# Attention with a look-ahead term and an FFN on one core: all rows of the squared pairs' probabilities turned by VectorE's squares and DRAM

## Chip, cores and metric

One core of a Trainium2 chip. The metric is the device time of one launch in microseconds, the median of several runs; lower is better. The engines are TensorE (matmuls and transposes, into PSUM), VectorE, ScalarE and GpSimd (elementwise work; GpSimd does not touch PSUM here) and SyncE, whose queue issues the DMA transfers. In the profile they are PE (PEld for its weight loads), DVE, ACT, POOL and SP (SPq for its queue). Each runs its own program in order and waits on semaphores.

## The reference

A layer norm, then attention with a look-ahead term and a gated FFN side by side, both added to x. There are 8 batches of 512 tokens of 256 features, 8 heads of 64.

```python
xn = _layernorm(x)
qu, ku, vu, qc, kc, vc = split_heads(xn @ W_qkv.T)      # 6 x (8, 8, 512, 64)
term1 = where(causal_mask, 0, (qc * SCALE) @ vu.T)
lookahead = where(causal_mask, sigmoid((qu * SCALE) @ ku.T), 0)
Su = term1 @ lookahead.T
scores = where(causal_mask, neg, (qc * SCALE) @ kc.T - silu(Su))
out = softmax(scores) @ vc
x = x + merge_heads(out) @ W_out.T + ffn(xn)            # ffn: silu(x @ wg) * (x @ wu) @ wd, hidden 768
```

## The kernel before, in words

Numbers are split in two parts of fewer bits each, HIGH and LOW (ScalarE copies a value to the rounded type, VectorE subtracts the copy from the value), and a product of two split numbers is three matmuls.

The attention is a pipeline of 32 **steps**, one for each pair of heads of a batch: step g = 4b + q. The function `step` exists once for each engine and is an order of work written out by hand. In step g TensorE computes, for pair g, the look-ahead products L (`look_ahead`), term1 T (`term1`) and their product Su (`sum_up`); for pair g-1 the scores (`scores`); for pair g-2 the output (`attend`); and the projections of pair g+1. The causal triangle of a head is cut in three groups, `ROWS = [(4,), (3, 1), (2,)]`: the row block of four 128-column blocks, then those of three and of one, then that of two. Each of L, T, scores and Su goes by these groups, j = 0, 1, 2.

What happens to pair g-1 in step g, row group by row group: VectorE forms minus the scores from PSUM and the gate and takes their least (`minus_scores`, L1487), into the tile `prob`; ScalarE takes the exponential and its sum (`exp_of`, L1176); VectorE the inverse of the sum (`inverse`, L1499); GpSimd multiplies by it (`norm`, L668). `attend` then wants these probabilities with keys along the partitions, that is transposed, split in HIGH and LOW, in the tile `PT_s`. There are two ways to this:

- The last row block (four blocks of columns, both heads) of the pairs below `SQUARED` = 30 goes by **squares and DRAM**: VectorE transposes every 32 x 32 square in place (`row_in_squares`, L1527), SyncE spreads the squares to DRAM (`spread_last_row`, L545, eight DMAs of 64 KB in pieces of 128 B), waits for them, and gathers them back as transposed blocks (L552, four DMAs). In the next step ScalarE and VectorE split them (`high_last_row`, L1204; `low_last_row`, L1533).
- The other three row blocks of these pairs are transposed by TensorE, six 128 x 128 transposes for a head (`turn_head`, L867), between the sums: one head behind sum 0 and one behind sum 1. ScalarE (`high_head`, L1196, L1198) and VectorE (`low_head`, L1521) split them out of PSUM behind the gate and its product of the same sum.

The last two pairs are turned wholly by TensorE (`turn_probs`, L842).

**The tail of a step.** TensorE runs sum 0, a head's transposes, sum 1, the other head's, sum 2. For each sum ScalarE takes a tanh (`gate_of`, L1168) and VectorE a product with the sum (`silu_of`, L1471), which frees the sum's banks in PSUM. Ahead of this VectorE has the LOW parts of L (`low_L`, L1457), of the projections (`low_proj`, L1419) and of the values (`low_values`, L1424), and by q: at q = 0 the statistics of the next x, at q = 1 its scaling and its transpose by squares, at q = 2 the LOW part of xT, at q = 3 nothing of these (a plain step). The weights of the FFN are split in chunks in steps 4 to 25.

**The banks.** PSUM has 8 banks, and `TURNS` lists which banks each piece of work takes, in the order in which TensorE takes them. `take_bank` makes TensorE wait until what was in them before is emptied. Sum 0 has banks 6 and 7, which the next step's first T takes; sum 1 has 2 and 3, which the first L takes.

```python
TURNS = [("Sc", 0, (0, 1)), ("L", 0, (2, 3)), ("K0", 0, (0,)), ("T", 0, (6, 7)), ("L", 1, (4, 5)), ("T", 1, (2, 3)),
```

`attend` of a pair below `SQUARED` waits for the LOW parts of a head (L878) and of the last row (L879). SyncE's program in a step is, in order: the spread of x at q = 2, the store and the load of a weight chunk, the loads of q = 0, then at the end the last row's spread and gathers and the store of the output of pair g-2. The loads for the FFN stand in the last two steps; the last batch's xT is loaded in step 31 (L530).

After the steps comes the FFN of all batches with the output projection, on TensorE `gate_up`, `down` and `project_o`. The change touches no work of it but three banks and that load.

Of the kernel before, what the change touches and what calls it, by code (L numbers as in the profile page):

```python
# [103 lines left out]
class LayerNorm:  # L104
# [35 lines left out]
    def scale(self, dve, b):  # L140

        sh = self.sh
        for n in range(TT):
# [18 lines left out]
         ("Su", 0, (6, 7)), ("PH", 0, (0, 1)), ("PT", 0, (0, 1)), ("PT", 1, (4,)), ("Su", 1, (2, 3)),  # L162
         ("PH", 1, (6, 7)), ("PT", 2, (6, 7)), ("Su", 2, (4, 5))]
# [44 lines left out]
def layer(nc, x, W_qkv, w_gate, w_up, w_down, W_out, w_split, xT_copy, xT_raw, prob_raw, sh, heads_out, out):  # L208
# [4 lines left out]
    with ctx:  # L213
# [36 lines left out]
        flat_prob = prob[:, :, :].rearrange("p h c -> p (h c)")  # L250
        flat_T = T_s[:, :, :, :].rearrange("p h a c -> p (h a c)")
# [60 lines left out]
        last_row_in_squares = sem("last_row_in_squares")  # L312
        last_row_spread = sem("last_row_spread")
        last_row_loaded = sem("last_row_loaded")
        last_row_high = sem("last_row_high")
        last_row_low = sem("last_row_low")
# [48 lines left out]
        def gate_up_bank(b, m):  # L365

            if b > 0:
                return double[m % 2]
            return bank("GU", m) if m < 3 else double[(0, 0, 3)[m - 3]]
# [43 lines left out]
        def after(g, j):  # L413
            return g * 3 + j + 1

        def turned(g, n):
            return g * 2 + n + 1 if g < SQUARED else SQUARED * 2 + (g - SQUARED) * 3 + n + 1
# [34 lines left out]
        def run_steps(b, part, step, count=STEPS):  # L452


            for q in range(count):
                g = b * STEPS + q
                step(part, b, q, g, q >= 1 or part != FIRST, q >= 2 or part != FIRST, q < 3 or part != LAST)

        @block.sync
        def _(sp):  # L460
# [45 lines left out]
            def step(part, b, q, g, back1, back2, ahead):  # L506
# [19 lines left out]
                if part == LAST and q == 3:  # L526
                    sp.wait_ge(proj_filled, proj_count(LAST_G, KC))
# [11 lines left out]
            def spread_last_row(g, attended):  # L539

                sp.wait_ge(last_row_in_squares, g + 1)
                sp.sem_inc(ticks, 1)
                for h in range(2):
                    for i in range(4):
                        sp.dma_start(prob_raw[g][h].rearrange("q r t -> r q t")[:, :, i * 32:(i + 1) * 32],  # L545
                                     prob[i * 32:(i + 1) * 32, h, 0:SEQ].rearrange("r (q t) -> r q t", t=32)) \
                          .then_inc(last_row_spread, 16)
                sp.wait_ge(last_row_spread, (g + 1) * 8 * 16)
                if attended:
                    sp.wait_ge(o_filled, 2 * g)  # L550
                for K, at in enumerate((3, 6, 9, 7)):
                    sp.dma_start(PT_blocks[:, :, LOW, at, :],  # L552
                                 prob_raw[g][:, 4 * K:4 * K + 4, :, :].rearrange("h q r t -> (q r) h t")) \
                      .then_inc(last_row_loaded, 16)
# [81 lines left out]
        def _(pool):  # L636
# [25 lines left out]
            def norm(g, j):  # L662

                wait_before(pool, inv_done, after(g, j))
                for h in range(2):
                    for w in ROWS[j]:
                        v = prob[:, h, WIDE[w]:WIDE[w] + w * P]
# [60 lines left out]
        def _(pe):  # L728
# [109 lines left out]
            def turn_row(out, h, w):  # L838

                K = TT - w  # L840
                for I in range(K, TT):
                    last = pe.transpose(out[:, (I - K) * P:(I - K + 1) * P],  # L842
                                        prob[:, h, WIDE[I + 1] + K * P:WIDE[I + 1] + (K + 1) * P], ident[:, :])
# [17 lines left out]
            def turn_head(part, b, g, h):  # L861

                if h == 0:
                    pe.wait_ge(prob_ready, after(g - 1, 2))
                tile = take_bank(part, b, g, "PH", h)
                for i, (K, I) in enumerate([(0, 0), (0, 1), (0, 2), (1, 1), (1, 2), (2, 2)]):
# [949 lines left out]
```

## Time and profile before

| | us |
|---|---|
| three runs, median (lowest to highest) | 1081.72 (1080.22 to 1082.07) |
| the profiled execution, and its span | 1082.21, 1080.2 |
| busy in the span: TensorE, its weight loads | 1058.2, 947.6 |
| VectorE, ScalarE, GpSimd | 871.9, 755.8, 567.1 |
| packets of DMA, of these under 512 B | 246076, 161232 |

The span is from the first to the last instruction of the profiled execution. A matmul's record overlaps its neighbours', so that a row of TensorE is best read by the starts: the start of the next group less its own. An instruction of another engine can likewise start before the end recorded for the one ahead of it. The duration of a DMA issue is the time in the queue that issues it and not the time of the transfer. The granted TensorE clock was 0.996 of full speed.

### The profile page before, as it was taken

The numbers are of one execution on the slowest core, as the hardware profiler recorded it, in microseconds if no ns is written. First come the engines' busy times: TensorE is split into PE (matmuls) and PEld (weight loads), VectorE is DVE, ScalarE is ACT, GpSimd is POOL, SyncE is SP. The second block draws the span as 40 slices with busy tenths as digits, with TensorE's granted clock in tenths as the row PEclk, the third lists the DMA queues.
The fourth block names the chain that finished last, engine by engine and source line by source line (L and its number), as shares of the span: only waits on it lengthen the run. The fifth ranks groups of instructions, "written<-read, shape, count | busy, mean of one in ns | idle before, by whom it ended". The sixth has DMA issues, their size and how long they took to land.

```text
span 1080.2 us, 21562 instructions
## 1 busy us (share of the span) xinstructions
PE 1058.2 (98%) x7652; PEld 947.6 (88%) x7652; DVE 871.9 (81%) x1831; ACT 755.8 (70%) x1483; POOL 567.1 (52%) x630
## 2 busy tenths in 40 slices
PE   6999999999999999999999999999999899999998
PEld 5888888888888888888888889988889888899997
DVE  5788789888988898889888988888777768667766
ACT  6678777877787778777877787778777755443333
POOL 5355565556555655565556555656555545422230
PEclk9999999999999999999999999999999989999999
DMA  5032434343434343344334343433324546556631
GB/s 195 1 79 64 118 89 110 76 104 102 91 96 101 105 101 86 91 116 89 99 77 130 79 109 76 125 79 80 98 59 123 161 144 237 175 179 217 214 133 60
DMA packets 246076, 120.72 MB, mean 112 GB/s; under 512 B 161232, under 2 KB 227024, under 8 KB 243920
## 3 DMA queue, kind: packets, MB, share of 16 engines
q1 hardware_dynamic: 245968, 119.31, 40.5%
q8 instruction: 63, 1.03, 0.4%
q14 instruction: 45, 0.37, 0.1%
HBM read 64.75 MB, written 54.53 MB: 110 GB/s over the span
## 4 chain that ended last, share of the span: by engine, by line
PE 89%; DVE 3%; ACT 2%; issue 2%; POOL 1%; DMA 1%; SPq 1%; DVEq 0%; POOLq 0%; ACTq 0%
PE X L833 23%; PE X L748 20%; PE X L986 7%; PE X L885 7%; PE X L977 7%; PE X L817 6%; PE X L801 5%; PE X L787 5%; PE X L772 4%; PE X L867 4%; POOL prob L668 1%; DMA xT<-xT_copy 1%; DVE L_s L1457 1%; ACT prob L1176 1%; ACT T_s L1154 1%
## 5 line engine op out<-in xcount | busy, mean ns | idle before, releaser
L668 POOL TENSOR_SCALAR prob<-prob,inv 128x512 f32<-128x512 f32 (+3 forms) x256 | 301.4, 1194 | 16.3 <-DVE inv L1499 16.3
L833 PE MATMUL X<-L_s,T_s 128*128 128x128 f32 (+3 forms) x1920 | 281.7, 301 | 2.0 <-DVE L_s L1457 2.0
L833 PEld LDWEIGHTS X<-L_s,T_s 128*128 128x128 f32 x1920 | 267.5, 189 | 13.4 <-issue 2.8
L748 PE MATMUL X<-xT,W 128*128 128x512 f32 (+1 forms) x972 | 244.8, 399 | 0.0
L748 PEld LDWEIGHTS X<-xT,W 128*128 128x128 f32 x972 | 175.7, 191 | 40.8 <-issue 0.4
L1168 ACT ACTIVATE gate<-X 128x1024 f32<-128x1024 f32 (+1 forms) x96 | 84.9, 884 | 154.7 <-PE X L833 154.7
L642 POOL TENSOR_SCALAR_AFFINE_SELECT gate<-gate 128x256 f32<-128x256 f32 (+1 forms) x96 | 47.5, 495 | 205.2 <-DVE gate L1471 205.2
L1471 DVE SCALAR_TENSOR_TENSOR gate<-gate,X 128x1024 f32<-128x1024 f32 (+1 forms) x96 | 99.6, 1038 | 64.0 <-ACT gate L1168 64.0
L658 POOL TENSOR_SCALAR_AFFINE_SELECT T_s<-T_s 128x512 fp32r<-128x512 f32 x128 | 104.6, 829 | 85.4 <-DVE T_s L1464 85.4
L1176 ACT ACTIVATE prob<-prob,least 128x512 f32<-128x512 f32 (+3 forms) x256 | 141.8, 587 | 1.5 <-DVE least L1487 1.5
L1487 DVE CUSTOM_DVE_ANT_0 prob<-X,gate 128x512 f32<-128x512 f32 (+3 forms) x256 | 112.8, 487 | 25.8 <-PE X L817 24.2
L1464 DVE TENSOR_TENSOR T_s<-X,T_s 128x1024 fp32r<-128x1024 f32 (+1 forms) x96 | 100.1, 1043 | 28.9 <-ACT T_s L1154 28.9
L1457 DVE SCALAR_TENSOR_TENSOR L_s<-tanh_l,L_s 128x1024 fp32r<-128x1024 f32 (+1 forms) x96 | 104.0, 1083 | 0.5 <-ACT L_s L1160 0.5
L1146 ACT ACTIVATE tanh_l<-X 128x1024 f32<-128x1024 f32 (+1 forms) x96 | 85.5, 890 | 23.3 <-PE X L787 23.2
L885 PEld LDWEIGHTS X<-PT_s,v_s 128*128 128x128 f32 x512 | 80.8, 188 | 10.2 <-DVE PT_s L1512 1.5
L1154 ACT ACTIVATE T_s<-X 128x1024 fp32r<-128x1024 f32 (+1 forms) x96 | 85.8, 893 | 4.5 <-PE X L801 4.5
L885 PE MATMUL X<-PT_s,v_s 128*128 128x512 f32 (+3 forms) x512 | 85.2, 319 | 1.7 <-DVE PT_s L1512 1.1
L1160 ACT ACTIVATE L_s<-tanh_l 128x1024 fp32r<-128x1024 f32 (+1 forms) x96 | 85.6, 938 | 0.0
L817 PE MATMUL X<-kc_s,qc_s 64*128 64x512 f32 (+3 forms) x768 | 84.6, 337 | 0.0
L801 PE MATMUL X<-qc_s,vu_s 64*128 64x512 f32 (+3 forms) x768 | 81.8, 327 | 0.0
L650 POOL TENSOR_SCALAR_AFFINE_SELECT tanh_l<-tanh_l 128x256 f32<-128x256 f32 (+1 forms) x96 | 54.0, 563 | 51.1 <-ACT tanh_l L1146 51.1
L787 PE MATMUL X<-qu_s,ku_s 64*128 64x512 f32 (+3 forms) x768 | 79.5, 319 | 0.5 <-ACT tanh_l L1146 0.3
(108 smaller groups left out, 1888.2 us busy)
## 6 DMA issues: line engine op xcount, KB each, us to landing
heads_out<-o_s SPq DMA_DIRECT2D x62, 256.0 KB, 3.3
prob_raw<-prob SPq DMA_DIRECT2D x240, 64.0 KB, 1.9
PT_s<-prob_raw SPq DMA_DIRECT2D x120, 128.0 KB, 2.4
xT_copy<-xT SPq DMA_DIRECT2D x8, 1024.0 KB, 6.8
w_split<-w_parts SPq DMA_DIRECT2D x22, 256.0 KB, 2.5
W<-w_split SPq DMA_DIRECT2D x12, 384.0 KB, 6.9
xT<-xT_copy SPq DMA_DIRECT2D x4, 1024.0 KB, 6.3
tanh_l<-in_L_attn_x SPq DMA_DIRECT2D x8, 512.0 KB, 4.9
```

What stands on the lines that cost most here:

```text
L658: last = pool.affine_select(out=v, in_=v.bitcast(F32), compare_op=ALU.is_ge, fill=0.0, base=0, pattern=[[0, 2], [0, 2], [1, P]], channel_m ...
L668: last = pool.tensor_scalar(v, v, inv[:, h, w - 1:w], None, ALU.mult)
L748: last = pe.matmul(out[:, tokens], sh.W[:, a, k, cols], xT[:, c, k, tokens], start=(n == 0), stop=(n == 3 * KD - 1))
L787: last = pe.matmul(both[:, h, at:at + w * P], ku_s[rows, a, J * P:(J + 1) * P], qu_s[rows, c, 0:w * P], start=(n == 0), stop=(n == 2))
L801: last = pe.matmul(both[:, h, at:at + w * P], vu_s[rows, a, J * P:(J + 1) * P], qc_s[rows, q % 2, c, J * P:SEQ], start=(n == 0), stop=(n = ...
L817: last = pe.matmul(both[:, h, at:at + w * P], qc_s[rows, par, a, I * P:(I + 1) * P], kc_s[rows, par, c, 0:w * P], start=(n == 0), stop=(n ...
L833: last = pe.matmul(both[:, h, at:at + (J + 1) * P], T_s[:, h, a, to:to + P], L_s[:, h, c, WIDE[J + 1]:WIDE[J + 1] + (J + 1) * P], start=(J ...
L885: last = pe.matmul(both[:, h, K * P:SEQ], v_s[:, slot // 4, K, slot % 4, :, :], PT_s[:, h, c, at:at + (TT - K) * P], start=(K == 0 and c = ...
L1176: last = act.activation(v, v, ACT.Exp, bias=least[:, h, w - 1:w], scale=-1.0, accum_out=total[:, h, w - 1:w])
L1457: dve.scalar_tensor_tensor(L_s[:, :, LOW, c:c + n], tanh_l[:, :, c:c + n], 1.0, L_s[:, :, HIGH, c:c + n].bitcast(F32), ALU.add, ALU.subtra ...
L1464: dve.tensor_tensor(T_s[:, :, LOW, c:c + n], bank("T", j)[:, :, 0:n], T_s[:, :, HIGH, c:c + n].bitcast(F32), ALU.subtract).then_inc(T_low, 1)
L1487: last = dve.tensor_tensor_reduce(prob[:, h, WIDE[w]:WIDE[w] + w * P], both[:, h, at:at + w * P], gate[:, h, WIDE[w]:WIDE[w] + w * P], SU_ ...
```

## The change

For the pairs below `SQUARED` all four row blocks go by squares and DRAM. `turn_head`, `high_head` and `low_head` are gone, and with them TensorE's transposes and the banks `PH`. The tile `prob` is laid out so that both heads' parts of a row group lie side by side (`prob_row`, `prob_rows`): 1024 columns for row 3, 768 for row 2, and 768 for rows 1 and 0 together.

VectorE transposes the three groups in turn (`row_in_squares(g, I)` for I = 3, 2, 1), each behind its own norm, at three places in its order. SyncE spreads groups 3 and 2; **ScalarE** issues the spread of the third group (I = 1), between its first and its second gate. Each spread is four DMAs. SyncE gathers all of them, ten DMAs. ScalarE and VectorE split the whole of `PT_s` in two instructions each, 1280 columns for a head (`high_rows`, `low_rows`), where they split the last row before. Sum 0 now has banks 2 and 3, sum 1 has 6 and 7. VectorE's LOW parts of the projections QU and KU move behind those of L. The last batch's xT is loaded in step 30, and `double[1]` and `double[3]` change places in the first FFN stage.

```diff
-         ("Su", 0, (6, 7)), ("PH", 0, (0, 1)), ("PT", 0, (0, 1)), ("PT", 1, (4,)), ("Su", 1, (2, 3)),
-         ("PH", 1, (6, 7)), ("PT", 2, (6, 7)), ("Su", 2, (4, 5))]
+         ("Su", 0, (2, 3)), ("PT", 0, (0, 1)), ("PT", 1, (4,)), ("Su", 1, (6, 7)),
+          ("PT", 2, (2, 3)), ("Su", 2, (4, 5))]
...
+        def prob_row(h, w):
+            return flat_prob[:, 2 * WIDE[w] + h * w * P:2 * WIDE[w] + (h + 1) * w * P]
+
+        def prob_rows(I):
+            return flat_prob[:, 1792:2 * TRI] if I == 1 else flat_prob[:, 2 * WIDE[I + 1]:2 * (WIDE[I + 1] + (I + 1) * P)]
...
+        def spread_row(eng, g, I):
+
+            eng.wait_ge(row_in_squares_done[I], g + 1)
+            eng.sem_inc(ticks, 1)
+            to = prob_raw[I][g].rearrange("q r t -> r q t")
+            for i in range(4):
+                eng.dma_start(to[:, :, i * 32:(i + 1) * 32],
+                             prob_rows(I)[i * 32:(i + 1) * 32, :].rearrange("r (q t) -> r q t", t=32)) \
+                  .then_inc(row_spread[I], 16)
...
                 if part == LAST and q == 3:
+                    load_down_out()
+                if part == LAST and q == 2:
+                    load_gate_up()
                     sp.wait_ge(proj_filled, proj_count(LAST_G, KC))
                     sp.wait_ge(v_filled, LAST_G + 1)
                     sp.wait_ge(xT_stored, BATCH * 16)
                     load_xT(0)
-                    load_down_out()
-                if part == LAST and q == 2:
-                    load_gate_up()
                 if back1 and g - 1 < SQUARED:
-                    spread_last_row(g - 1, back2)
+                    for I in (3, 2):
+                        spread_row(sp, g - 1, I)
+                    if back2:
+                        sp.wait_ge(o_filled, 2 * g - 2)
+                    for I in (3, 2, 1):
+                        gather_row(g - 1, I)
                 if back2:
                     store_o(g - 2, q % 2)
...
+            def gather_row(g, I):
+
+                sp.wait_ge(row_spread[I], (g + 1) * 4 * 16)
+                for i in (I, 0) if I == 1 else (I,):
+                    for K in range(i + 1):
+                        sp.dma_start(PT_blocks[:, :, LOW, WIDE[TT - K] // P + i - K, :], raw_row(g, i)[:, 4 * K:4 * K + 4, :, :].rearrange("h q r t -> (q r) h t")) \
+                          .then_inc(row_loaded[I], 16)
...
                     if g - 2 < SQUARED:
-                        pe.wait_ge(PT_low, turned(g - 2, h))
-                        pe.wait_ge(last_row_low, 2 * (g - 2) + 2)
+                        pe.wait_ge(rows_low, 2 * (g - 2) + h + 1)
...
                 sum_up(part, b, g, 0)
-                if back1 and g - 1 < SQUARED:
-                    turn_head(part, b, g, 0)
-                elif back1:
+                if back1 and g - 1 >= SQUARED:
                     turn_probs(part, b, g, 0)
                     turn_probs(part, b, g, 1)
                 sum_up(part, b, g, 1)
-                if back1 and g - 1 < SQUARED:
-                    turn_head(part, b, g, 1)
-                elif back1:
+                if back1 and g - 1 >= SQUARED:
                     turn_probs(part, b, g, 2)
                 sum_up(part, b, g, 2)
...
+            def high_rows(g):
+
+                for I in (3, 2, 1):
+                    act.wait_ge(row_loaded[I], (g + 1) * (I + 1 if I > 1 else 3) * 16)
+                for h in range(2):
+                    act.activation(PT_s[:, h, HIGH, :], PT_plain[:, h, LOW, :], ACT.Copy).then_inc(rows_high, 1)
...
                 if back2 and g - 2 < SQUARED:
-                    high_last_row(g - 2)
+                    high_rows(g - 2)
...
                 gate_of(g, 0)
                 if back1 and g - 1 < SQUARED:
-                    high_head(g - 1, 0)
-                elif back1:
+                    spread_row(act, g - 1, 1)
+                if back1 and g - 1 >= SQUARED:
                     high_PT(g - 1, 0)
                     high_PT(g - 1, 1)
                 gate_of(g, 1)
...
+                if 0 <= g - 1 < SQUARED:
+                    for I in ((3,), (2, 1), (1,))[j]:
+                        wait_before(dve, row_spread[I], g * 4 * 16)
...
+            def row_in_squares(g, I):
+
+                dve.wait_ge(prob_ready, after(g, 3 - I))
+                dve.transpose(prob_rows(I), prob_rows(I)).then_inc(row_in_squares_done[I], 1)
+
+            def low_rows(g):
+
+                for h in range(2):
+                    dve.wait_ge(rows_high, 2 * g + h + 1)
+                    dve.tensor_tensor(PT_s[:, h, LOW, :], PT_plain[:, h, LOW, :], PT_plain[:, h, HIGH, :], ALU.subtract) \
+                       .then_inc(rows_low, 1)
...
                 if back1:
                     inverse(g - 1, 1)
-                if ahead:
-                    low_proj(g + 1, QU, par)
                 low_L(g, 1)
-                if ahead:
-                    low_proj(g + 1, KU, par)
...
                 if back1:
                     inverse(g - 1, 2)
+                if ahead:
+                    low_proj(g + 1, QU, par)
+                    low_proj(g + 1, KU, par)
                 if back1 and g - 1 < SQUARED:
-                    row_in_squares(g - 1)
+                    row_in_squares(g - 1, 3)
                 if ahead:
                     low_proj(g + 1, VU, par)
+                if back1 and g - 1 < SQUARED:
+                    row_in_squares(g - 1, 2)
...
+                if back1 and g - 1 < SQUARED:
+                    row_in_squares(g - 1, 1)
                 if 0 <= g - FIRST_CHUNK < INT_CHUNKS:
                     take_low_max(g - FIRST_CHUNK)
```

## Rows read from the trace of the kernel before

**Rows 1.** The page, engines: busy us (share of the span) xinstructions.

```profile
PE 1058.2 (98%) x7652; PEld 947.6 (88%) x7652; DVE 871.9 (81%) x1831; ACT 755.8 (70%) x1483; POOL 567.1 (52%) x630
```

**Rows 2.** The waits: who waited for whom, us in total, times, longest.

```profile
PE X L977 <- DMA xT<-xT_copy: 3.6, 1, 3.6
```

**Rows 3.** TensorE's timeline over one plain step: start us, us, what.

```profile
421.59 0.97 PE L817 MATMUL X<-kc_s,qc_s 64*128 64x512 f32 x6
...
439.06 3.95 PE L833 MATMUL X<-L_s,T_s 128*128 128x512 f32 x24
442.84 0.84 PE L867 MATMUL X<-ident,prob 128*128 128x128 f32 x6
443.44 3.30 PE L833 MATMUL X<-L_s,T_s 128*128 128x384 f32 x24
446.58 0.84 PE L867 MATMUL X<-ident,prob 128*128 128x128 f32 x6
...
448.67 0.96 PE L817 MATMUL X<-kc_s,qc_s 64*128 64x512 f32 x6
...
450.20 0.96 PE L801 MATMUL X<-qc_s,vu_s 64*128 64x512 f32 x6
```

**Rows 4.** Windows: length, busy us by engine (x), PEclk, DMA share, GB/s.

```profile
448.67:475.74 27.07, 27.07 (x203) 24.28 (x202) 23.70 (x58) 20.95 (x42) 16.75 (x19) 1.00 0.52 142
475.74:503.04 27.30, 27.23 (x204) 24.34 (x204) 24.72 (x54) 20.96 (x42) 15.76 (x18) 1.00 0.28 65
```

**Rows 5.** Groups by line and shape: busy us, mean ns | idle before.

```profile
L1457 DVE SCALAR_TENSOR_TENSOR L_s<-tanh_l,L_s 128x1024 fp32r<-128x1024 f32 x64 | 82.3, 1285 | 0.5 <-ACT L_s L1160 0.5
...
L1160 ACT ACTIVATE L_s<-tanh_l 128x1024 fp32r<-128x1024 f32 x64 | 65.0, 1085 | 0.0
...
L1527 DVE STREAM_TRANSPOSE prob<-prob 128x1024 f32<-128x1024 f32 x30 | 36.6, 1220 | 0.0
```

**Rows 6.** VectorE's timeline: last row's split, tails and gate products of three steps.

```profile
431.54 1.53 DVE L1533 TENSOR_TENSOR PT_s<-PT_s 128x768 fp32r<-128x768 f32 x2
...
438.06 0.68 DVE L1457 SCALAR_TENSOR_TENSOR L_s<-tanh_l,L_s 128x512 fp32r<-128x512 f32 x1
...
442.31 0.39 DVE L1439 TENSOR_REDUCE low_max<-w_parts 128x1 f32<-128x256 f32 x1
...
447.90 1.22 DVE L1471 SCALAR_TENSOR_TENSOR gate<-gate,X 128x1024 f32<-128x1024 f32 x1 [1.58 <-ACT gate L1168]
449.04 1.02 DVE L1521 TENSOR_TENSOR PT_s<-X,PT_s 128x512 fp32r<-128x512 f32 x2
...
471.73 1.21 DVE L1471 SCALAR_TENSOR_TENSOR gate<-gate,X 128x1024 f32<-128x1024 f32 x1
...
499.65 1.20 DVE L1471 SCALAR_TENSOR_TENSOR gate<-gate,X 128x1024 f32<-128x1024 f32 x1
```

**Rows 7.** ScalarE's timeline: a step's second gate, and the last row's copies.

```profile
446.84 1.03 ACT L1168 ACTIVATE gate<-X 128x1024 f32<-128x1024 f32 x1 [1.95 <-PE X L833]
...
483.45 1.18 ACT L1204 ACTIVATE PT_s<-PT_s 128x768 fp32r<-128x768 f32 x2
```

**Rows 8.** GpSimd's timeline: the norms of the second and third group.

```profile
435.88 6.27 POOL L668 TENSOR_SCALAR prob<-prob,inv 128x384 f32<-128x384 f32 x6 [0.57 <-DVE inv L1499]
```

**Rows 9.** SyncE's timeline: a spread, four gathers, and the spread of x.

```profile
440.10 4.20 SPq L545 DMA_DIRECT2D prob_raw<-prob  x8
...
472.78 1.91 SPq L552 DMA_DIRECT2D PT_s<-prob_raw  x4
...
504.52 4.12 SPq L499 DMA_DIRECT2D xT_raw<-xb  x4
```

**Rows 10.** The source line of the spread: issue in ns, min/median/max.

```profile
L545 SPq DMA_DIRECT2D prob_raw<-prob x240: 303/496/2047, 60.2 to 851.2; - x120
```

**Rows 11.** The DMA view, issues: count, KB each, median us from issue to landing.

```profile
PT_s<-prob_raw SPq DMA_DIRECT2D x120, 128.0 KB, 2.4
...
xT_raw<-xb SPq DMA_DIRECT2D x28, 128.0 KB, 3.8
```

More of the change, by code:

```diff
@@ L311, in layer @@
         prob_ready = sem("prob_ready")
[L312 to L316, printed above, removed]
+        row_in_squares_done = {I: sem(f"row{I}_in_squares") for I in (3, 2, 1)}
+        row_spread = {I: sem(f"row{I}_spread") for I in (3, 2, 1)}
+        row_loaded = {I: sem(f"row{I}_loaded") for I in (3, 2, 1)}
+        rows_high = sem("rows_high")
+        rows_low = sem("rows_low")
         PT_high = sem("PT_high")
@@ L859, in turn_probs @@
                 last.then_inc(PT_filled, 1)
[L861 to L866, printed above, removed]
-                    last = pe.transpose(tile[:, i // 3, i % 3 * P:(i % 3 + 1) * P],
-                                        prob[:, h, WIDE[I + 1] + K * P:WIDE[I + 1] + (K + 1) * P], ident[:, :])
-                last.then_inc(PT_filled, 1)
             def attend(part, b, q, g, both=None):
@@ L1029, in ffn_first @@
                 pe.wait_ge(scores_emptied, after(LAST_G, 1))
-                gate_up(0, 5, products, double[3])
+                gate_up(0, 5, products, double[1])
                 for m in range(5):
@@ L1377, in step @@
                 gate_of(g, 1)
-                if back1 and g - 1 < SQUARED:
-                    high_head(g - 1, 1)
-                elif back1:
+                if back1 and g - 1 >= SQUARED:
                     high_PT(g - 1, 2)
@@ L1486, in minus_scores @@
                         at = WIDE[w] - GROUP[j][0]
-                        last = dve.tensor_tensor_reduce(prob[:, h, WIDE[w]:WIDE[w] + w * P],
+                        last = dve.tensor_tensor_reduce(prob_row(h, w),
                                                         both[:, h, at:at + w * P],
@@ L1512, in low_PT @@
                 dve.tensor_tensor(out, src, high.bitcast(F32), ALU.subtract).then_inc(PT_low, 1)
-            def low_head(g, h):
-                dve.wait_ge(PT_high, turned(g, h))
-                src = bank("PH", h)
-                for at, part in ((0, lambda a: PT_blocks[:, h, a, 0:8, :].rearrange("p (n i) c -> p n (i c)", n=2)[:, :, 0:2 * P]),
-                                 (2 * P, lambda a: PT_blocks[:, h, a, 2:9:6, :])):
-                    n = 2 * P if at == 0 else P
-                    last = dve.tensor_tensor(part(LOW).bitcast(F32R), src[:, :, at:at + n], part(HIGH), ALU.subtract)
-                last.then_inc(PT_low, 1)
-            def row_in_squares(g):
-                dve.wait_ge(prob_ready, after(g, 0))
-                dve.transpose(prob[:, :, 0:SEQ], prob[:, :, 0:SEQ]).then_inc(last_row_in_squares, 1)
-            def low_last_row(g):
-                for i, at in enumerate((slice(3, 10, 3), slice(7, 8))):
-                    dve.wait_ge(last_row_high, 2 * g + i + 1)
-                    dve.tensor_tensor(PT_blocks[:, :, LOW, at, :].bitcast(F32R), PT_blocks[:, :, LOW, at, :],
-                                      PT_blocks[:, :, HIGH, at, :], ALU.subtract).then_inc(last_row_low, 1)
+            def row_in_squares(g, I):
[6 more added lines that the diff above has]
+                       .then_inc(rows_low, 1)
             def first_stats(h):
@@ L1605, in ffn_first @@
                 low_h(0, 0)
[L1606 removed]
+                minus_scores(LAST_G, 0, double[3])
                 gated_of(0, 3)
                 hidden(0, 3)
[L1609 removed]
+                minus_scores(LAST_G, 1, double[1])
                 low_h(0, 1)
@@ L1756, in step @@
                 silu_of(g, 0)
-                if back1 and g - 1 < SQUARED:
-                    low_head(g - 1, 0)
-                elif back1:
+                if back1 and g - 1 >= SQUARED:
                     low_PT(g - 1, 0)
@@ L1762, in step @@
                 silu_of(g, 1)
-                if back1 and g - 1 < SQUARED:
-                    low_head(g - 1, 1)
-                elif back1:
+                if back1 and g - 1 >= SQUARED:
                     low_PT(g - 1, 2)
@@ L1790, in build @@
     xT_raw = [nc.dram_tensor(f"xT_raw{b}", [TT, 8, 32, P], F32).ap() for b in range(BATCH)]
-    prob_raw = [nc.dram_tensor(f"prob_raw{g}", [2, 16, 32, P], F32).ap() for g in range(SQUARED)]
+    prob_raw = {I: [nc.dram_tensor(f"prob_raw{I}_{g}", [2 * (4 * I + 4 if I > 1 else 12), 32, P], F32).ap() for g in range(SQUARED)] for I in (3, 2, 1)}
     heads_out = nc.dram_tensor("heads_out", [2, BATCH * INNER, SEQ], F32).ap()
```

58 lines of the change are left out of this document (17 added, 41 removed).

## The prediction

> **What bounds the kernel now.** I read the page's engine totals first: TensorE is busy for 1058.2 of 1080.2 us [rows 1]. Then the waits: TensorE's own longest is 3.6 us, once, for a load near the end [rows 2]. Then one step in TensorE's order of time [rows 3]: group after group with no gap, 27.08 us from one first score matmul (421.59) to the next (448.67). The windows give 27.07 and 27.30 for the two steps behind it, with VectorE busy for 23.70 and 24.72 of them [rows 4]. The reader is to see that what leaves TensorE's row shortens every step by as much, until another engine's result is late. So the question is what is late next. I count time t from a step's first score matmul (421.59, 448.67, 475.74).
>
> **What goes.** A head's six transposes stand between two sums, 442.84 to 443.44, and the other head's from 446.58, as many again [rows 3]. Thirty steps have two such places: 60 x 0.60 = 36.0 us. The shortest step is then 27.08 - 1.20 = 25.88. The steps that scale and turn x are 0.2 longer now [rows 4]; I let 7 x 0.2 = 1.4 go too, with the tiles that made the sum wait. The last batch's xT is now loaded a step earlier, which takes away the 3.6 us of [rows 2]. Gain on the path: 41.0.
>
> **VectorE.** Removed: four subtractions of the heads, 1.02 for a head's two, twice, and 1.53 for the last row's two [rows 6]: 3.6. Added: two squares of 768 columns, by the 1220 ns of 1024 columns 0.92 each, 0.87 behind one another; and two subtractions of 1280 columns in SBUF, by the 1285 of 1024 columns 1.6 each [rows 5]: 5.0. Net +1.4 us a step on an engine with 2.6 to 3.4 free [rows 4]: it fits, with little left. Place matters more than the total. The long subtractions come 1.6 later than now ahead of the L parts, but two pieces of 0.6 (QU, KU) move behind those, so L's last part ends at t = 17.2 against 17.07 now (438.06 + 0.60 [rows 6]), and the sum starts at 17.47 (439.06 [rows 3]): hidden, by 0.3. Behind it come the two moved pieces (1.2), two squares (1.74) and that 0.1: everything up to the gate's product is 3.05 later. Now the tail ends at t = 21.1 in the plain step (442.31 + 0.39), and the product starts at 23.06 (471.73) in the step with statistics and at 23.91 (499.65) in the one that scales and turns x [rows 6]. New: 24.1, 26.1, 26.95. The third square, the reduction's 0.32 ahead of these, ends at 23.8, 25.8, 26.6.
>
> **ScalarE's compute.** Two copies that took 1.18 go and two of 1280 columns come, by the 1085 ns of 1024 columns 1.3 each: +1.3 ahead of L's high parts [rows 5, 7]. L's last high part then ends near t = 16.4, inside the 17.2 above. The four copies of the heads go too; they stood where the DMA issues now stand, so they free no place on the path of their own, and I cost that at nothing.
>
> **ScalarE's four DMA issues.** This term decides. The third group's spread waits for the third square, and behind it in ScalarE's queue stands the gate of the second sum. That sum now ends at t = 24.4 (17.47 + 3.78 + 3.14 [rows 3]), and ScalarE would start the gate at once. From the gate's start to the end of VectorE's product it is 2.3 us (446.84 to 447.90 + 1.22 [rows 6, 7]), and the next step's first T matmul, 1.53 in (450.20 [rows 3]), writes the banks that this product frees (6 and 7). With D for the four issues the product ends at 23.8 + D + 2.3 in a plain step; T wants the banks at 25.88 + 1.53 = 27.4. TensorE stalls D - 1.3 in 17 steps (the plain ones and those that split xT, whose extra work on VectorE stands behind the third square), D + 0.7 in six with statistics, D + 1.5 in seven that scale and turn: 30D - 22.1 + 4.2 + 10.5 = 30D - 7.4 in all.
>
> No issue from ScalarE is in the trace. SyncE's issue of 512 pieces of 128 B took 303 ns at the least and 496 in the middle [rows 10], eight of them 4.20 us; four of 1024 pieces took 4.12 [rows 9]. Ours have 768 pieces. Low end: 4 x 0.303 = 1.2. By the middle of the smaller kind: 2.1. By the larger kind, 4.12 x 0.75 = 3.1. I take 3.1, the nearest in load: those four, like ours, ran into DMA engines that had other transfers (the store of o stood just ahead of them), and 0.75 of 1024 is the same size as ours. High end: SyncE spreads the first two groups from t = 19.8 to about 27, over the whole of ours in a plain step; shared 1.5 times over D is 4.6, and 1.7 times 5.3.
>
> A page speaks to this. The Trainium skill (DMA: Bandwidth & Descriptors, Issuing engines are not separate DMA queues) says that issuing from several engines at once only saves the sequencer's time, and that this is usually small beside the transfer. The trace disagrees on "small": four issues took 4.12 us for transfers that land 3.8 us after each [rows 9, 11]. By the page ScalarE's term would vanish; that is the first rival below.
>
> **SyncE's and GpSimd's queues.** SyncE had 8 spreads and 4 gathers in a step. Now it has four spreads of 128 KB (4.2 us), four of 96 KB (3.1), ten gathers at 0.48 (4 took 1.91 [rows 9]) behind three waits, and the store of o last. From t = 19.8: spreads to 27.2, first gathers to 29.1, second to 30.8, third to 32.2; the last, issued at 31.7, lands 2.4 later [rows 11] at 34.1. ScalarE's copy of the rows stands at t = 7.7 of the next step (483.45 [rows 7]), so a step shorter than 34.1 - 7.7 = 26.4 waits for them. At the forecast's length they are early by a microsecond or more. The store and the next step's chunk may slip a little; they are wanted a step later. GpSimd keeps its work: its six norms take 6.27 us [rows 8], the second group's share some 4.5, from t = 15.3 to 19.8, and the second square wants them at 20.3: hidden by 0.5.
>
> **Sum.** 30 x 3.1 - 7.4 = +85.6 us of stall against -41.0: +44.6. On the profiled execution's 1082.2 (2.0 around its span of 1080.2) this is 1126.8; the median of the runs shown, 1081.7, is 0.5 lower, so I say 1126.
>
> **Rivals.** *ScalarE's issues are cheap, and the change is faster.* At D = 0 only VectorE is late: its two products take 2.35, so they end at 25.4 + 2.35 = 27.75, 28.45 and 29.3 in the steps that split xT, take statistics, and scale: stalls of 7 x 0.35 + 6 x 1.05 + 7 x 1.9 = 22.1, in all -18.9; SyncE's floor of 26.4 gives back up to 8 over the plain steps: 1063 to 1071. At D = 1.2: 28.6 - 41.0 = -12.4, 1070. For it: the 303 ns, and a queue of ScalarE's own that is empty. Against: the middle of 240 issues is 496 [rows 10], and eight in a row never come to 8 x 0.303.
>
> *The spreads share the engines.* D is 4.6 to 5.3, and the last gathers land near t = 36, so the copy of the rows comes late as well: +89.6 to +110.6, 1172 to 1193. For it: by the times above they overlap in the plain step. Against: in the loaded steps the third square is 2 to 3 us later, when most of SyncE's second spread is out.
>
> *Stalls and gain cancel.* 30D - 7.4 = 41.0 at D = 1.6, issues of 0.4 each: between the rows, and narrow.
>
> The mechanism of the slower side is one: the second gate behind the four issues, from D = 1.6 up.
>
> **How the numbers follow.** The forecast, with D from 2.1 to 4.2, has 0.57 and a range of its own of 1097 to 1160. Issues cheap, 1063 to 1075: 0.25. Cancel: 0.04. Shared engines: 0.14. A measurement of this kernel can tell about 0.2% (2.2 us) from no change, so faster has 0.25, same 0.03 and slower 0.72. The range leaves out most of the last case and the best of the cheap one: 1065 to 1172.
>
> **What would show it.** In the new profile no transposes stand between the sums. TensorE is idle ahead of the first T group, released by VectorE's gate product: some 1.8 us in plain steps and 4.6 in those that scale x, so steps of 27.7 and 30.5. ScalarE stands four issues of 0.8 us ahead of the second gate. A first sum that still starts at t = 17.5 shows VectorE's moved work as hidden. If the second gate starts at t = 24.5, or the issues take 0.3 or less, the forecast is wrong and the first rival holds. If ScalarE's copy of the rows waits for the gathers, the cause is SyncE's queue, and the stall shows ahead of the first sum.

## The result, and the profile after

Four runs of the changed kernel took 1147.47, 1161.88, 1161.75 and 1146.21 us, median 1154.61; four of the kernel before beside them have the median 1081.89. The ratio is 1.0679 (1.0632 to 1.0725): the change makes the kernel slower by 73 us. The forecast was 1126, the range 1065 to 1172. The two runs above 1160 had a mean granted clock of 0.965, the other two 0.975 and 0.974. What is read below is the profiled run of 1147.47, 65.3 above the 1082.21 of the profiled execution before.

The page's engine totals of the kernel after, and its group lines of the waits ahead of TensorE's T groups (L820), ScalarE's gates (L1172) and VectorE's squares (L1513), columns as in [rows 1, 5]:

```profile
span 1145.5 us, 21052 instructions
PE 1051.1 (92%) x7292; PEld 927.0 (81%) x7292; DVE 914.0 (80%) x1771; ACT 743.9 (65%) x1363; POOL 592.2 (52%) x630
...
L1172 ACT ACTIVATE gate<-X 128x1024 f32<-128x1024 f32 (+1 forms) x96 | 81.5, 881 | 241.0 <-PE X L852 132.0
...
L820 PE MATMUL X<-qc_s,vu_s 64*128 64x512 f32 (+3 forms) x768 | 89.0, 350 | 58.0 <-DVE gate L1465 58.0
...
L1513 DVE STREAM_TRANSPOSE prob<-prob 128x768 f32<-128x768 f32 (+1 forms) x90 | 94.9, 1055 | 11.4 <-POOL prob L687 11.4
```

TensorE was busy for all but 22.0 us of its span [rows 1]; now it is idle for 94.4. Its own waits say where:

```profile
PE X L820 <- DVE gate L1465: 58.0, 30, 3.0
PE X L852 <- DVE kc_s L1413: 16.3, 13, 1.7
...
PE X L852 <- DVE L_s L1451: 2.8, 1, 2.8
```

The first did not exist in [rows 2]. It is the wait that the forecast put ahead of T: once in each of 30 steps, up to 3.0 us. The second, "the wait for KC" below, stands ahead of the last of the three sums: L1413 is VectorE's LOW part of the projection KC, which empties bank 4, one of that sum's two. The 3.6 for xT is gone.

One step of the kernel after on TensorE, in order of time, from the first score matmul (452.74) to the next (480.30), to be held against [rows 3]:

```profile
452.74 0.97 PE L836 MATMUL X<-kc_s,qc_s 64*128 64x512 f32 x6
453.87 0.96 PE L806 MATMUL X<-qu_s,ku_s 64*128 64x512 f32 x6 [0.16 <-DVE gate L1465]
455.94 0.97 PE L820 MATMUL X<-qc_s,vu_s 64*128 64x512 f32 x6 [1.11 <-DVE gate L1465]
...
471.88 8.50 PE L852 MATMUL X<-L_s,T_s 128*128 128x512 f32 x60
480.30 0.97 PE L836 MATMUL X<-kc_s,qc_s 64*128 64x512 f32 x6
...
483.69 0.96 PE L820 MATMUL X<-qc_s,vu_s 64*128 64x512 f32 x6 [1.72 <-DVE gate L1465]
```

The 60 matmuls of the three sums are now one row without a gap: the transposes are gone. T starts 3.20 and 3.39 behind the step's first score matmul, where it started 1.53 behind it [rows 3].

What ScalarE, VectorE and SyncE do in this step's tail, in order of time:

```profile
475.98 1.03 ACT L1172 ACTIVATE gate<-X 128x1024 f32<-128x1024 f32 x1 [2.32 <-PE X L852]
478.74 2.42 ACTq L478 DMA_DIRECT2D prob_raw<-prob  x4
481.26 1.51 ACT L1172 ACTIVATE gate<-X 128x1024 f32<-128x1024 f32 x2 [4.25 <-PE X L852]
```

```profile
475.00 0.98 DVE L1513 STREAM_TRANSPOSE prob<-prob 128x768 f32<-128x768 f32 x1 [0.41 <-POOL prob L687]
...
477.67 0.96 DVE L1513 STREAM_TRANSPOSE prob<-prob 128x768 f32<-128x768 f32 x1
...
482.32 1.82 DVE L1465 SCALAR_TENSOR_TENSOR gate<-gate,X 128x1024 f32<-128x1024 f32 x2 [2.26 <-ACT gate L1172]
```

```profile
474.11 5.71 SPq L478 DMA_DIRECT2D prob_raw<-prob  x8
479.92 6.39 SPq L572 DMA_DIRECT2D PT_s<-prob_raw  x10
```

The chain is to be read across the first two fences: the third square ends at 478.63, ScalarE's four issues run from 478.74 to 481.16, the second gate starts at 481.26, and T at 483.69, 2.5 behind the issues. The page's "issue" or "PE X" beside a gate is only the last releaser by the profile; the row of the four issues right ahead of the gate is what held it. ScalarE's queue, not its arithmetic, sets the step.

### The profile page after: what moved, and what is told of

Read it like the earlier page. It is cut to its first block, busy times and chain, and to the rows that moved or that the text cites. A ratio compares the mean times of both kernels' runs of the same rounds, so it can differ in the third digit from the quotient of the medians.

```text
span 1145.5 us, 21052 instructions
## 1 busy us (share of the span) xinstructions
PE 1051.1 (92%) x7292; PEld 927.0 (81%) x7292; DVE 914.0 (80%) x1771; ACT 743.9 (65%) x1363; POOL 592.2 (52%) x630
## 4 chain that ended last, share of the span: by engine, by line
PE 36%; DVE 29%; POOL 15%; issue 6%; ACTq 6%; ACT 6%; DMA 1%; SPq 1%; DVEq 0%; POOLq 0%
POOL prob L687 11%; PE X L767 8%; DVE PT_s L1519 8%; PE X L990 7%; ACTq L478 6%; PE X L981 6%; PE X L820 5%; DVE prob L1513 5%; PE X L836 4%; PE X L806 3%; DVE gate L1465 3%; POOL T_s L677 3%; ACT gate L1172 3%; DVE prob L1483 2%; PE X L852 2%
## 5 line engine op out<-in xcount | busy, mean ns | idle before, releaser
L687 POOL TENSOR_SCALAR prob<-prob,inv 128x512 f32<-128x512 f32 (+3 forms) x256 | 320.1, 1266 | 1.3 <-DVE inv L1495 0.8
L852 PE MATMUL X<-L_s,T_s 128*128 128x128 f32 (+3 forms) x1920 | 278.3, 304 | 19.4 <-DVE kc_s L1413 16.3
L1172 ACT ACTIVATE gate<-X 128x1024 f32<-128x1024 f32 (+1 forms) x96 | 81.5, 881 | 241.0 <-PE X L852 132.0
L1465 DVE SCALAR_TENSOR_TENSOR gate<-gate,X 128x1024 f32<-128x1024 f32 (+1 forms) x96 | 96.8, 1035 | 76.4 <-ACT gate L1172 76.4
L820 PE MATMUL X<-qc_s,vu_s 64*128 64x512 f32 (+3 forms) x768 | 89.0, 350 | 58.0 <-DVE gate L1465 58.0
L820 PEld LDWEIGHTS X<-qc_s,vu_s 64*128 64x128 f32 x768 | 68.1, 202 | 72.4 <-issue 71.7
L1513 DVE STREAM_TRANSPOSE prob<-prob 128x768 f32<-128x768 f32 (+1 forms) x90 | 94.9, 1055 | 11.4 <-POOL prob L687 11.4
L1519 DVE TENSOR_TENSOR PT_s<-PT_s 128x1280 fp32r<-128x1280 f32 x60 | 94.5, 1614 | 0.0
L806 PE MATMUL X<-qu_s,ku_s 64*128 64x512 f32 (+3 forms) x768 | 88.4, 348 | 0.9 <-DVE gate L1465 0.5
L836 PE MATMUL X<-kc_s,qc_s 64*128 64x512 f32 (+3 forms) x768 | 88.9, 350 | 0.0
```

The lines of the kernel that those rows point to most:

```text
L687: last = pool.tensor_scalar(v, v, inv[:, h, w - 1:w], None, ALU.mult)
L820: last = pe.matmul(both[:, h, at:at + w * P], vu_s[rows, a, J * P:(J + 1) * P], qc_s[rows, q % 2, c, J * P:SEQ], start=(n == 0), stop=(n = ...
L836: last = pe.matmul(both[:, h, at:at + w * P], qc_s[rows, par, a, I * P:(I + 1) * P], kc_s[rows, par, c, 0:w * P], start=(n == 0), stop=(n ...
L852: last = pe.matmul(both[:, h, at:at + (J + 1) * P], T_s[:, h, a, to:to + P], L_s[:, h, c, WIDE[J + 1]:WIDE[J + 1] + (J + 1) * P], start=(J ...
L1465: dve.scalar_tensor_tensor(gate[:, :, c:c + n], gate[:, :, c:c + n], 1.0, bank("Su", j)[:, :, 0:n], ALU.add, ALU.mult).then_inc(silu_done, 1)
L1513: dve.transpose(prob_rows(I), prob_rows(I)).then_inc(row_in_squares_done[I], 1)
```

## The experiments

Eight kernels ran. The runs of the kernel before beside the first four (third_by_sync, no_third_spread, fill, third_by_tensor) have the median 1081.68, those beside the others 1080.12.

### No third spread, no issue on ScalarE

```diff
-                if back1 and g - 1 < SQUARED:
-                    spread_row(act, g - 1, 1)
```

Besides, the gathers of rows 1 and 0 read the first group's squares, and wait for SyncE's spread of the second group. Left out of the computation: the DRAM trip of rows 1 and 0, whose values are then other ones; VectorE still makes the third square, and the ten gathers stay.

> The changed kernel without ScalarE's four issues and without the third group's spread; the third square is still made and the third gathers read the first group's squares instead (the blocks of rows 1 and 0 are not this pair's). Theory (the second gate behind ScalarE's issues): the issues' 2.3 us a step go, T's stall falls to what VectorE's later products leave, some 30 us in all instead of 83, and the clock's falls go with the long stalls: 1075 to 1090. Rival (VectorE's later third square and products hold T, whoever issues): at most 15 us less, 1130 or more.

Measured: 1077.22, ratio 0.9955 (0.9941 to 0.9969). The end of its step with statistics and the start of the next, on TensorE and on ScalarE:

```profile
472.96 1.57 PE L852 MATMUL X<-L_s,T_s 128*128 128x256 f32 x12 [0.91 <-DVE kc_s L1411]
474.46 0.96 PE L836 MATMUL X<-kc_s,qc_s 64*128 64x512 f32 x6
476.40 0.98 PE L820 MATMUL X<-qc_s,vu_s 64*128 64x512 f32 x6 [0.17 <-DVE gate L1463]
```

```profile
472.14 1.02 ACT L1172 ACTIVATE gate<-X 128x1024 f32<-128x1024 f32 x1 [2.09 <-PE X L852]
```

With the issues gone the gate starts as soon as the sum is there, and T's wait is 0.17, where the same step of the kernel after has 2.70. The rest of the change is worth 4.5 us; with the third spread on ScalarE the time is 70 higher than here (1147.5 - 1077.2, or 77 by the medians). The wait for KC stands here too (13 times, 16.4 us in all), and so does the 0.40 of the second square: those are VectorE's and GpSimd's, not the issues'. This kernel leaves out the third spread's transfers too; the next one keeps them.

The mean granted clock was 0.989. In five steps, each behind a KC wait of 1.6, the first matmuls of the step ran at half speed, as here (502.58, behind the wait of the step that scales x); the score group above took 0.96:

```profile
502.58 1.36 PE L836 MATMUL X<-kc_s,qc_s 64*128 64x512 f32 x6
503.74 1.49 PE L806 MATMUL X<-qu_s,ku_s 64*128 64x512 f32 x6
505.02 1.48 PE L820 MATMUL X<-qc_s,vu_s 64*128 64x512 f32 x6
```

Those steps took 27.3 us, the sixth of their kind, at full speed, 26.3.

### The third spread on SyncE

```diff
-                    for I in (3, 2):
+                    for I in (3, 2, 1):
                         spread_row(sp, g - 1, I)
...
-                if back1 and g - 1 < SQUARED:
-                    spread_row(act, g - 1, 1)
```

> The changed kernel with the third spread issued by SyncE behind the other two. Theory: T's stall falls to under 1 us in plain steps, but SyncE's queue, whose last gathers land just in time for ScalarE's copy of the rows now, is 2.6 us longer, so that copy waits and the stall stands ahead of the first sum instead, a floor of 29.5 us a step: 1130 to 1160. Rival (SyncE's queue has room): 1075 to 1090 as without the third spread.

Measured: 1125.25, ratio 1.0412 (1.0387 to 1.0437): 22 us better than the change's two better runs (29 by the medians), a little below the 1130 to 1160 that was expected, and still 44 worse than before. ScalarE's copy of the rows and TensorE behind it:

```profile
480.03 2.44 ACT L1201 ACTIVATE PT_s<-PT_s 128x1280 fp32r<-128x1280 f32 x2 [2.15 <-DMA PT_s<-prob_raw]
```

```profile
483.11 2.80 PE L893 MATMUL X<-PT_s,v_s 128*128 128x512 f32 x16 [1.01 <-DVE PT_s L1517]
489.88 7.14 PE L852 MATMUL X<-L_s,T_s 128*128 128x512 f32 x48 [1.10 <-DVE L_s L1449]
```

The stall has moved from T to `attend` and the first sum: SyncE issues twelve spreads ahead of ten gathers, the last gather lands late, and ScalarE's copy, with L's HIGH parts behind it, waits 54.5 us in all. In the kernel after that wait is 0.4 us, once. T's own wait is 1.8 us in all, with the same twelve spreads going to DRAM as in the kernel after: what held T there was the place of the issues in ScalarE's queue, and not the traffic. At neither of these two places do four more DMAs a step fit without a stall.

### ScalarE's issues behind the second gate, and behind all three

```diff
-                if back1 and g - 1 < SQUARED:
-                    spread_row(act, g - 1, 1)
...
                 gate_of(g, 1)
+                if back1 and g - 1 < SQUARED:
+                    spread_row(act, g - 1, 1)
```

> The changed kernel with ScalarE's four issues moved behind the second gate, ahead of the third. Theory: the second gate starts as its sum ends, T waits for VectorE alone; the third gate is late by the issues instead, and its banks are wanted by the second L group 0.8 us behind T, so about half of the stall stays: 1115 to 1135, the stall now ahead of that L group. Rival (ScalarE's queue as a whole is too full, the place is nothing): 1145 or more.

> The changed kernel with ScalarE's four issues moved behind all three gates. Theory: T and L have their banks in time; the next step's tanh and copies start 2.3 us late instead, and with them L's last part, which has 0.3 us to spare ahead of the first sum: a stall of 1 to 2 us there, 1105 to 1130. Rival (the place is nothing): 1145 or more.

Measured: behind the second gate 1109.31, ratio 1.0261 (1.0241 to 1.0282), better than expected; behind the third 1138.80, ratio 1.0548 (1.0525 to 1.0570), worse than expected. Behind the second gate, on ScalarE and TensorE:

```profile
465.56 1.03 ACT L1172 ACTIVATE gate<-X 128x1024 f32<-128x1024 f32 x1 [2.09 <-PE X L852]
465.65 2.33 ACTq L478 DMA_DIRECT2D prob_raw<-prob  x4
468.08 0.60 ACT L1172 ACTIVATE gate<-X 128x512 f32<-128x512 f32 x1 [1.50 <-issue]
...
476.10 2.44 ACT L1201 ACTIVATE PT_s<-PT_s 128x1280 fp32r<-128x1280 f32 x2 [1.09 <-DMA PT_s<-prob_raw]
```

```profile
485.95 7.14 PE L852 MATMUL X<-L_s,T_s 128*128 128x512 f32 x48 [1.02 <-DVE L_s L1451]
```

The same four issues (2.33 us) stand one instruction later, and T's wait of 58.0 us is gone (2.8 left). Part of them costs nothing here: they start 0.09 behind the second gate and run beside it for the 0.94 us that it still takes, and then until the third sum ends. The third gate starts 1.32 behind the next step's first score matmul (466.76), where it starts 0.17 behind it in the kernel without the issues (474.63 and 474.46). Two smaller waits are there instead of the 58.0: 15.2 us ahead of L for the third gate's product, and 18.2 ahead of the first sum, since the third group now reaches DRAM later and the copy waits 1.09 for it. Behind all three gates the issues stand ahead of the tanh of L, and TensorE says so:

```profile
481.62 1.08 PE L820 MATMUL X<-qc_s,vu_s 64*128 64x384 f32 x12 [2.05 <-ACT tanh_l L1150]
```

That wait, 25.2 us in all, is what I had not counted. Three places in one queue gave 1154.6, 1109.3 and 1138.8: what stands behind an issue in its queue decides its price, 45 us from one gate to the next. A part of the 45 is the clock, whose mean is 0.991 to 0.995 behind the second gate and 0.965 to 0.975 in the change; the next experiment is about that part.

### TensorE's work in the stall

L's first group is computed three times in steps 2 to 31, with the same result: 1.4 us more of matmuls a step, 43 in all, just ahead of the T that stalls.

```diff
-                for w in ROWS[j]:
+                for again in range(REPEAT if j == 0 and 2 <= g <= SQUARED + 1 else 1):
+                  for w in ROWS[j]:
```

> The changed kernel with the first L group computed three times over in steps 2 to 31 (same result, 1.4 us more TensorE work a step, 43 us in all, put just ahead of T's wait). Theory (the idle stretch ahead of T costs the clock, 15 us or more in all, on top of the stall itself): the granted clock rises from 0.975 to 0.99 or more and the time falls to 1125 to 1140, although TensorE works more. Rival (the half clock has another cause): clock as it was and 1147 to 1165. Second rival (TensorE's work bounds these steps): 1147 + 43.

Measured: 1131.10, ratio 1.0453 (1.0435 to 1.0470); clocks of 0.987, 0.998, 0.988 and 0.991. Forty-three us of work were added and the kernel became 16 us faster than the change's better runs. If the idle time only absorbed them the time would have stayed at 1147; what it gave back is time at the lower clock. The same three groups (T of the row of four, L and T of the row of three) in the kernel after behind a wait of 2.77 and behind one of 1.11, in the windows:

```profile
426.90:430.90 4.00, 3.98 (x30) 3.80 (x32) 2.93 (x7) 2.15 (x3) 1.02 (x2) 0.58 0.47 132
455.90:459.20 3.30, 3.27 (x42) 3.25 (x43) 2.91 (x7) 2.60 (x4) 1.01 (x2) 1.00 0.74 207
```

The third number from the end is the granted clock: 0.58 against 1.00. Ahead of the first window TensorE had been idle for 1.63 and then 2.77 us:

```profile
420.88 1.57 PE L852 MATMUL X<-L_s,T_s 128*128 128x256 f32 x12 [1.63 <-DVE kc_s L1413]
...
426.92 1.65 PE L820 MATMUL X<-qc_s,vu_s 64*128 64x512 f32 x6 [2.77 <-DVE gate L1465]
428.34 1.73 PE L806 MATMUL X<-qu_s,ku_s 64*128 64x384 f32 x12
```

From the T group to the next score group it is 3.98 here (426.92 to 430.90) and 2.44 in the other (455.94 to 458.38). Eight of the 31 steps of the kernel after show such a place, with 12.5 us above 2.44 in all, and the kernel with the fill shows one (1.2 us). From the first score matmul of step 1 to that of step 32 the kernel after takes 912.6 us and the one with the fill 898.5; 13.0 of these 14.1 us lie in those eight steps. The clock part of the expectation, at least 0.99, held in two runs of four only: less idle time makes the fall to 1.2 GHz rarer, it does not exclude it. Nor does each fall cost time: the runs at 0.998 and at 0.988 took 1129.88 and 1129.93. In the profiled one six of the falls come behind a wait for KC and slow a step's score and L groups; these steps take 28.1 to 29.1 us, and the one of their kind without a fall 28.9. T had to wait anyway.

### The last batch's xT alone

The kernel before, with nothing but the load of xT moved from step 31 to step 30.

```diff
                 if part == LAST and q == 3:
+                    load_down_out()
+                if part == LAST and q == 2:
+                    load_gate_up()
                     sp.wait_ge(proj_filled, proj_count(LAST_G, KC))
...
-                    load_down_out()
-                if part == LAST and q == 2:
-                    load_gate_up()
```

> The kernel before with only the last batch's xT loaded in step 30 instead of step 31. Theory: TensorE's 3.6 us wait for it goes, and nothing else moves: 1077 to 1079 beside 1081.7. Rival (another load or wait ends just behind it): 1081 to 1082.

Measured: 1076.41, ratio 0.9962 (0.9948 to 0.9976), 3.7 us for the 3.6 of [rows 2], a little under the 1077 expected. The last step with attention takes 29.24 in place of 33.90, 4.66 less. More than the wait is gone from it: in the kernel before the clock fell behind that wait, and eight matmuls took 3.78 us (the first line), which take 2.11 here (861.30). In the kernel after the step takes 37.58, since waits of 2.31 for the gate's product and 2.77 for L's LOW part (the last line of the fence of waits above) stand in it, with the lower clock behind each; behind the second the first sum takes 6.77 us (the second line) for 4.01 here (872.74).

```profile
865.06 3.78 PE L977 MATMUL X<-xT,W 128*128 128x512 f32 x8 [3.60 <-DMA xT<-xT_copy]
...
939.64 6.77 PE L852 MATMUL X<-L_s,T_s 128*128 128x512 f32 x24 [2.77 <-DVE L_s L1451]
```

### Only two groups by DRAM, the third by TensorE

The kernel after, with no issue on ScalarE: rows 1 and 0 of both heads go by six transposes behind the first sum, 180 in the place of the 360 of before. The second of these two kernels also splits what came from DRAM head by head, and empties QC's bank ahead of the second square.

```diff
+            def turn_head(part, b, g):
+                pe.wait_ge(prob_ready, after(g - 1, 2))
+                tile = take_bank(part, b, g, "PH", 0)
+                for h in range(2):
+                    for i, (K, I) in enumerate([(0, 0), (0, 1), (1, 1)]):
+                        last = pe.transpose(tile[:, h, i * P:(i + 1) * P], prob_row(h, I + 1)[:, K * P:(K + 1) * P], ident[:, :])
+                last.then_inc(PT_filled, 1)
...
-                    for I in (3, 2, 1):
+                    for I in (3, 2):
                         gather_row(g - 1, I)
...
-                    spread_row(act, g - 1, 1)
+                    high_head(g - 1)
```

> A version between the two: the first and second groups (rows 3 and 2) go by squares and DRAM, the third (rows 1 and 0, three blocks a head) by six transposes of TensorE behind the first sum; no DMA of ScalarE, one square less on VectorE. Theory: TensorE's step is 27.08 - 0.60, saving 18 us, and the earlier load saves 3.6; VectorE's tail is 2.1 us later than before, which stalls T only in the steps that scale x, 5 us: about 1065, 1055 to 1075. Rival (the second group by DRAM alone already makes VectorE or SyncE late in every step): 1085 or more.

> The version between the two again, with its two stalls taken out: the rows are split head by head, so that the output's first head no longer waits for both (0.4 to 0.5 us a step there), and VectorE empties QC ahead of the second square and of the scaling of x (TensorE's transposes waited 1.2 us for QC's bank in the steps that scale). Theory: both stalls go, 30 x 0.4 and 7 x 1.2, about 20 us: 1057 to 1063. Rival (VectorE, now later by the extra instructions, stalls the first sum or T instead): 1070 or more.

Measured: the first 1080.30 (one of its ten executions took 2566.84, for which nothing here gives a cause), ratio 0.999 (0.998 to 1.000), not the 1065 that was expected. The profile had the reason: `attend` waits for a split that comes for both heads at once, and the transposes for QC's bank, in all 10.7 and 9.0 us.

```profile
PE X L903 <- DVE PT_s L1541: 10.7, 29, 0.7
PE X L886 <- DVE qc_s L1433: 9.0, 7, 2.0
```

With both mended the second took 1072.06, ratio 0.9922 (0.9905 to 0.9938): 8.1 us faster than the kernel before and 82 faster than the change, and still 9 above what was expected. What is late now is the LOW part of the transposed rows ahead of the next score matmuls:

```profile
PE X L836 <- DVE PT_s L1553: 8.6, 13, 0.8
```

Its plain steps take 26.6, against 27.1 before; some 4 of its 8 us are the earlier xT, by the run above. Its granted clock is 0.999. It is the best version found.

## Why the prediction came out as it did

**The bound and the mechanism: right.** TensorE's row set the time, and every gap in it now is a late result of another engine, the four issues ahead of the second gate above all. The kernel without them is 4.5 us faster than before, with them 73 slower. The rival in which spreads share the engines is not what happened: the four issues took 2.2 to 2.75 us in most steps and 3.39 at the most, not 4.6 or more, and the gathers' lateness cost 0.4 us once.

**The gain: right in size.** The 60 places of 0.60 are gone, and the wait for xT gave 3.7 by itself. But that 3.6 did not come off the sum: waits of 2.31 and 2.77 in the same step, and the lower clock behind them, took its place.

**VectorE's L part and ScalarE's copies: right.** The first sum starts 19.14 behind the step's start, 17.47 without that step's own delay of 1.67 ahead of T; the forecast had 17.47 and 17.5. Its 17.2 for the end of L's last part does not follow from the terms it gives, though: 17.07 + 1.6 - 1.2 is 17.5, with no cover left. The trace has 17.1 (471.55 - 452.74 - 1.67), since VectorE had waited 0.52 for ScalarE's exponentials ahead of the inverses of the second group (435.33 in the kernel before), and does not any more. The subtractions of 1280 columns took 1614 ns (forecast 1.6), by form:

```profile
L1519 DVE TENSOR_TENSOR PT_s<-PT_s 128x1280 fp32r<-128x1280 f32 x60 | 94.5, 1614 | 0.0
```

**The third square: 0.4 late.** Reckoned the same way it ends at 24.2, not at 23.8, because the second square waits 0.41 for GpSimd's norms. I had cost that cover at nothing with 0.5 to spare; the six norms take 6.88 us where they took 6.27 [rows 8]:

```profile
469.89 6.88 POOL L687 TENSOR_SCALAR prob<-prob,inv 128x384 f32<-128x384 f32 x6
```

**The issues, D: too high, with a sum that hides it.** I took 3.1 for four; they took 2.42 in the step shown, 2.57 on the mean of the 30, and 589 ns each in the middle. That is above the middle of the smaller kind (496 [rows 10]) and below the 3.1 scaled from the larger kind. At D = 2.42 the forecast's 30D - 7.4 would be 65, at 2.57 it would be 70. What the trace shows: by the starts (T's in a step, less 1.53) T comes 68.1 us late in steps 2 to 30. Of this the record calls 56 idle ahead of T and L (58.0 and 0.5, less the last step's 2.31). The rest is 0.1 to 0.4 in most steps (3.39 - 1.53 = 1.86 where the row says 1.72, and 1.67 where it says 1.11 and 0.16) and 1.2 to 1.4 in the five whose first groups ran at half speed ahead of T. With 16.3 for KC this is some 84 in all, against 85.6. The smaller D is made up for by the square's 0.4 and by what the second product adds behind the issues, 2.5 in place of 2.3. The two errors cancelled; that the sum of the stalls is right is luck in part.

**The wait for KC: a place I missed.** In the steps with statistics and with scaling I had charged VectorE's lateness to T. About half of it (0.92 of 2.0 us and 1.62 of 2.8) fell ahead of the last part of the sums instead, where KC's bank is taken. It moves the step's end and takes as much off T's wait, so it changes the place and little of the size here. But it sets off a fall of the clock of its own, as the kernel without the third spread showed: five steps of 27.3 in place of 26.3. With plain steps of 26.0 to 26.6, which T's small wait holds above 25.9, that kernel stayed at 1077 where the forecast for D = 0 said 1063 to 1071.

**The clock: the step that failed.** The forecast left every matmul at full speed, although the trace before already had a fall behind its one long wait (the 3.78 above). Long waits drop the granted clock to its lower level, 1.2 GHz, and matmuls after them run at half speed. In the profiled run that is 12.5 us in the T and L groups; the fill's 16 us is a second reading of about the same. The page on TensorE in the Trainium skill (TensorE: Matmul & The Clock Gate, HAM oscillation — how this bites in real kernels) warns of this, that idle gaps in a kernel throttle it again and the work behind them pays. The trace agrees, at 0.58 in the window above.

The sum for the profiled run: -36.0 and -1.4 for the transposes, +84 of stalls, +11 (12.5 without the last step's 1.6) to 16 of clock, and the last step's +3.7 (37.58 against 33.90): 61 to 66, against 65.3 measured. The two runs at 1162 had a lower clock by 0.010 and are 15.0 longer than the other two on the mean; 0.010 of 1160 is 11.6 us (an estimate). No trace of them was taken, and whether the clock explains all of it, and why it would fall more often in them, stays open.

**The issue beside the transfer.** The Trainium skill (DMA: Bandwidth & Descriptors, Issuing engines are not separate DMA queues) says that issuing from several engines saves only the sequencer's time. The trace agrees: a spread issued by ScalarE lands no sooner, 3.9 us after its issue, where one by SyncE lands after 2.8. That this time is "usually small" holds for one issue, 0.59 us beside 3.9, and misleads here: four of them in front of a gate turn a gain of 4.5 us into a loss of 73.

## What to carry to other kernels

Price a DMA issue by what stands behind it in the queue of the engine that issues it: four issues of 0.6 us on ScalarE cost 2.4 us a step where the gate behind them freed a bank, and the same four one instruction later cost 45 us less over the kernel, in part because they then ran beside a gate and the clock fell less. When a forecast puts a stall of over 2 us in each step in a stream of matmuls, add what the clock takes on top. Before a whole path is moved off the bounding engine, try a part of it that the queues have room for: two groups of three gave 8 us where all three lost 73.

## What was not expected of the hardware

Idle time and clock are not in proportion. In the kernel after, waits ahead of T of 1.83 (twice) and of 2.31 to 2.77 were followed by the lower level, and others of 2.70, 2.77 and 2.97 were not; without the third spread waits of 1.6 were followed by it in five steps of six. So were five of the six waits for KC of 1.62 to 1.65 in the kernel after, where it cost little: T's wait took the slow groups in. The mean granted clock of a whole run (0.975) doesn't tell that a few short places carry the loss; the row lengths of one group, compared step by step, do.

GpSimd's multiplication of 384 columns took 1514 ns in the kernel before and 1919 here, by form:

```profile
L687 POOL TENSOR_SCALAR prob<-prob,inv 128x384 f32<-128x384 f32 x64 | 122.8, 1919 | 1.3 <-DVE inv L1495 0.8
```

It is 1901 without the spread, and 1627 in the kernels with the third group on TensorE, so it comes with the reordered work and not with the issues. The Trainium skill (GPSIMD Engine Reference, Specifications) has GpSimd share its SBUF interfaces with VectorE, in contention with its instructions that have two SBUF inputs. The trace agrees in part. The slow one of the two in a step took 2.69 us (from 469.89), and VectorE made L's LOW parts, with two SBUF inputs, beside it for 1.73 of them. But in the kernel before one took only 1.24 us (from 435.88) with such a part beside it for 0.94. The new subtractions are not the reason: they end at 467.63. No run here isolates it.
